# Layer 3's attention of a four-layer transformer stack: two units to a round instead of one

## The reference

```
xn = layer_norm(context) ; ln = layer_norm(latents)          # latents: the normalized x
q  = ln @ Wq                  (8 heads of 64)
k_x, v_x = xn @ Wkv           # k_x is turned by the rotary tables (cos, sin)
k_l, v_l = ln @ Wkv
k, v = concat(k_x, k_l), concat(v_x, v_l)                     # 512 keys
attn = softmax(q k^T / 8)
out  = (attn v) @ Wo
x = x + tanh(g) * out
```

## Time and profile before

| | |
|---|---|
| median of 3 runs | 1868.87 us (1865.15 to 1870.61) |
| the profiled execution's own time | 1862.23 us |
| its span | 1860.5 us |
| TensorE busy | 1693.1 us, 91% of the span |
| VectorE busy | 1091.3 us, 59% |
| ScalarE busy | 681.6 us, 37% |
| mean granted TensorE clock | 0.975 |

### The profile page before, as it was taken

One profiled execution on the slowest core, in us unless ns is written; L12 is line 12 of the kernel. 1 busy time (PEld: TensorE's weight loads), 2 busy tenths in 40 slices (PEclk: granted clock), 3 DMA queues, 4 the chain that ended last, 5 costly groups with the idle time before them and its releaser, 6 DMA issues. The chain is left out here.

```text
span 1860.5 us, 28250 instructions
## 1 busy us (share of the span) xinstructions
PE 1693.1 (91%) x9431; PEld 1236.4 (66%) x9431; DVE 1091.3 (59%) x3250; ACT 681.6 (37%) x1747; POOL 258.4 (14%) x277
## 2 busy tenths in 40 slices
PE   6889778799998999999887799999889999999799
PEld 4667546567766568888676578887656665656575
DVE  5988866568787532232368571002356777676666
ACT  5877842454454211111133222221133443344331
POOL 2100131211022100000232120000120001010115
PEclk9999989999999999999899899999989999999999
DMA  8854042211012325454353875335221111011363
GB/s 250 254 184 134 7 128 68 80 37 36 28 58 81 110 90 170 153 165 169 102 170 117 292 285 176 114 124 176 57 86 43 43 44 50 26 35 29 103 190 113
DMA packets 170926, 212.91 MB, mean 114 GB/s; under 512 B 17081, under 2 KB 137506, under 8 KB 170658
## 3 DMA queue, kind: packets, MB, share of 16 engines
q1 hardware_dynamic: 159730, 183.57, 30.7%
q0 software_dynamic: 10496, 27.28, 4.6%
q10 hardware_dynamic: 560, 0.27, 0.1%
HBM read 148.95 MB, written 57.92 MB: 111 GB/s over the span
## 5 line engine op out<-in xcount | busy, mean ns | idle before, releaser
L788 POOL DMA_INDIRECT slots_in<-f_xn,f_slot x88 | 85.0, 966 | 465.1 <-DVE f_slot L562 441.3
L3506 PE MATMUL r_bank<-r_w,r_hT 128*128 x624 | 139.3, 379 | 1.0 <-DVE r_hT L3650 1.0
L3506 PEld LDWEIGHTS r_bank<-r_w,r_hT 128*128 128x128 f32 x624 | 118.4, 190 | 22.8 <-issue 7.5
L1498 ACT ACTIVATE a_probs<-a_s,a_negmax 128x512 f32<-128x512 f32 x128 | 86.9, 684 | 103.7 <-DVE a_negmax L1746 103.7
L1347 PEld LDWEIGHTS a_t<-kept_ident,a_probs 128*128 128x128 f32 x768 | 83.1, 142 | 61.8 <-issue 38.8
L1331 PE MATMUL a_s<-a_kT,a_qT 64*128 64x256 f32 (+1 forms) x512 | 109.1, 524 | 14.2 <-ACT a_probs L1504 7.6
L3591 DVE TENSOR_TENSOR r_y<-r_bank,r_b_row 128x256 f32<-128x256 f32 (+1 forms) x27 | 14.7, 543 | 177.5 <-PE r_bank L3506 177.2
L3121 PE MATMUL r_bank<-r_xgT,r_firsts 128*128 128x256 f32 x512 | 113.2, 379 | 0.0
L2283 DVE CUSTOM_DVE_ANT_0 a_s<-a_s,a_mask_bias 128x256 f32<-128x256 f32 x256 | 100.5, 454 | 20.3 <-PE a_s L2110 20.1
L1746 DVE TENSOR_REDUCE a_negmax<-a_s 128x1 f32<-128x512 f32 x128 | 82.2, 683 | 49.7 <-PE a_s L1331 49.1
L1347 PE MATMUL a_t<-kept_ident,a_probs 128*128 128x128 f32 x768 | 106.4, 281 | 2.0 <-DVE a_probsT L1764 1.6
(11 more groups left out here) (424 smaller groups left out, 3408.3 us busy)
## 6 DMA issues: line engine op xcount, KB each, us to landing
r_firsts<-in_f_w SPq DMA_DIRECT2D x27, 1024.0 KB, 5.1
r_firsts<-in_f_w SPq DMA_DIRECT2D x46, 512.0 KB, 4.3
slots_in<-a_zeros SPq DMA_DIRECT2D x8, 2048.0 KB, 12.6
half_in<-a_zeros SPq DMA_DIRECT2D x8, 1024.0 KB, 9.7
r_w<-in_f_w SPq DMA_DIRECT2D x8, 1024.0 KB, 7.0
a_share_of<-shares_out SPq DMA_DIRECT2D x28, 256.0 KB, 3.9
r_xg<-slots_in SPq DMA_DIRECT2D x28, 256.0 KB, 2.9
slots_out<-r_y SPq DMA_DIRECT2D x28, 256.0 KB, 2.1
```

Source lines behind the costliest of these rows:

```text
L788: pool.indirect_dma_start(self.slots_in[:, :], bass.IndirectOffsetOnAxis(ap=self.slot[:, c, tile:tile + 1], axis=0), src, None).then_inc(s ...
L1498: last = nc.scalar.activation(probs[:, g % PROBS, i, :], bank[:, :], ACT.Exp, bias=negmax[:, g % 4, i, 0:1], accum_out=sum_of(e, h, t_only))
L3506: last = nc.tensor.matmul(d_bank[:, t * D:(t + 1) * D], hT[:, j % 2, m, t * P:(t + 1) * P], slots.second[:, bass.ds(e, 1), m, :], start=(m ...
```

## The change

In layer 3 two steps make a round. In a round TensorE issues the score products of both units (four in a row), then the turns of both units (s - 2 and s - 1), then the preparations, finishing parts and extras of the first step and of the second, then the value product. VectorE keeps maxima and copies unit by unit (maxima of s, copies of s - 2, maxima of s + 1, copies of s - 1) and does the other jobs of both steps after them. ScalarE does the exponentials of both units first. It gets one wait more: the second unit's exponentials wait for the turn of the unit that used the buffer of probabilities. Bank numbers follow the new order. The table of preparations changes: `rope` from position 1 to 2, `x` from 3 to 2, `v` 0 from 2 to 4 and `v` 1 from 3 to 4, `q` from 4 to 5, `kl` from 5 to 6, `v` 2 from 6 to 7. `x_ask` then lands at position 0 and `norm_x` at 1; the routing's `f_ask` at 0, `f_normed` at 1, `f_turn` at 2. The unit whose copies ScalarE takes over in each batch is unit 1 instead of unit 0. `rotate` moves from position 4 to 6. Choice, gates and count come later by 1, 1 and 2 steps; for the last routed group by 3, 3 and 4, with its tables at steps 64 to 67 instead of 61 to 64. Layer 1 has STRIDE 1 and keeps its order.

```
+    STRIDE = 2 if WIDE else 1
+    SOON_LAG, LOGITS_LAG, EXP_LAG, COUNT_LAG = (2, 4, 6, 3) if WIDE else (1, 3, 4, 2)
-    TURN_AT = U_OF["rope"] + 3 if cfg.rope else None
+    TURN_AT = U_OF["rope"] + 4 if cfg.rope else None
...
-        s = out_step(b) + (ASK_LAG if b < ASKED_SOON else 1)
+        s = out_step(b) + (ASK_LAG if b < ASKED_SOON else SOON_LAG)
...
-        extra[s + 3].append(("f_logits", b, 0))
+        extra[s + LOGITS_LAG].append(("f_logits", b, 0))
...
-        s = out_step(b1 - 1) + (1 if soon else ASK_LAG) + 4
+        s = out_step(b1 - 1) + (SOON_LAG if soon else ASK_LAG) + EXP_LAG
...
+    ROUNDS = [range(s, min(s + STRIDE, STEPS)) for s in range(0, STEPS, STRIDE)]
...
 # TensorE
+            for together in ROUNDS:
+                for s in together:
+                    if s < BATCH * NU:
+                        scores(*divmod(s, NU))
+                for s in together:
+                    if 0 <= s - LAG_T < BATCH * NU:
+                        turn_probs(*divmod(s - LAG_T, NU))
+                for s in together:
+                    b, u = divmod(s, NU)
+                    for kind, e, n in prep_jobs(b, u):
+                        prepare(kind, e, n)
...
+                for s in together:
+                    if 0 <= s - LAG_PV < BATCH * NU:
+                        weigh(*divmod(s - LAG_PV, NU), s)
...
 # ScalarE
+                    if s < BATCH * NU:
+                        if s != together[0] and s >= PROBS:
+                            act.wait_ge(t_full, t_at["pT", (s - PROBS) // NU, ((s - PROBS) % NU, 1)] + 1)
+                        exponent(*divmod(s, NU))
...
 # preparations of layer 3
-             {0: [("c", 0)], 1: [("rope", 0), ("rope", 1)], 2: [("v", 0)], 3: [("x", 0), ("v", 1)],
-              4: [("q", 0), ("q", 1)], 5: [("kl", 0), ("kl", 1)], 6: [("v", 2)], 7: [("v", 3)]},
+             {0: [("c", 0)], 2: [("x", 0), ("rope", 0), ("rope", 1)], 4: [("v", 0), ("v", 1)],
+              5: [("q", 0), ("q", 1)], 6: [("kl", 0), ("kl", 1)], 7: [("v", 2), ("v", 3)]},
```

More of the change, by code:

```diff
@@ L924, in tiled_attention @@
             extra[(e - 2) * NU + 3].append(("x_scale", e, 0))
-    COUNT_LAG = 2
     ON_ACT = {e * NU + U_OF["rope"] + 1 - LAG_T for e in range(1, BATCH)} if cfg.rope else set()
-    TURN_AT = U_OF["rope"] + 3 if cfg.rope else None
+    TURN_AT = U_OF["rope"] + 4 if cfg.rope else None
     ASK_LAG = (X_AT - 2 - LATEST) % NU if head is not None else 1
+    STRIDE = 2 if WIDE else 1
+    SOON_LAG, LOGITS_LAG, EXP_LAG, COUNT_LAG = (2, 4, 6, 3) if WIDE else (1, 3, 4, 2)
     ASKED_SOON = route.cfg.sparse - 1 if route.cfg.sparse < BATCH else route.cfg.last - 1
     for b in range(route.cfg.last):
-        s = out_step(b) + (ASK_LAG if b < ASKED_SOON else 1)
+        s = out_step(b) + (ASK_LAG if b < ASKED_SOON else SOON_LAG)
         extra[s].append(("f_ask", b, 0))
@@ L962, in tiled_attention @@
         number(kind, e, n)
[L963 to L977, removed]
+    for together in ROUNDS:
+        for s in together:
+            b, u = divmod(s, NU)
+            if b < BATCH:
+                s_at["qk", b, (u, 0)] = len(s_at)
+                s_at["qk", b, (u, 1)] = len(s_at)
+            if 0 <= s - LAG_T < BATCH * NU:
+                bb, uu = divmod(s - LAG_T, NU)
+                t_at["pT", bb, (uu, 0)] = len(t_at)
+                t_at["pT", bb, (uu, 1)] = len(t_at)
+        for s in together:
+            b, u = divmod(s, NU)
+            for kind, e, n in prep_jobs(b, u) + finish_jobs(b, u):
+                if kind not in ("share", "inverse"):
+                    number(kind, e, n)
+            for kind, e, n in extra[s]:
+                if kind in ("f_turn", "f_logits", "f_count"):
+                    number(kind, e, n)
     moved_at = {}
@@ L1412, in _ @@
                 pe.wait_ge(v_cleared, 1)
[L1413 to L1441, removed]
@@ new lines, in _ @@
+            for together in ROUNDS:
+                for s in together:
+                    if s < BATCH * NU:
+                        scores(*divmod(s, NU))
+                for s in together:
+                    if 0 <= s - LAG_T < BATCH * NU:
+                        turn_probs(*divmod(s - LAG_T, NU))
+                for s in together:
+                    b, u = divmod(s, NU)
+                    for kind, e, n in prep_jobs(b, u):
+                        prepare(kind, e, n)
+                    for kind, e, t in finish_jobs(b, u):
+                        if kind == "oback":
+                            turn_back(e, t)
+                        elif kind == "sums":
+                            turn_sums(e)
+                        elif kind == "spread":
+                            spread_inverse(e, t)
+                        elif kind == "y":
+                            project_out(e, t)
+                    for kind, e, n in extra[s]:
+                        if kind == "f_turn":
+                            route.tensor_turn(pe, s_turn(s_at[kind, e, n]), e).then_inc(s_full, 1)
+                        elif kind == "f_logits":
+                            if e == 0:
+                                pe.wait_ge(route.consts_in, 16 * len(route.consts))
+                            pe.wait_ge(s_free, s_at["f_turn", e, 0] + 1)
+                            route.tensor_logits(t_turn(t_at[kind, e, n]), e).then_inc(t_full, 1)
+                        elif kind == "f_count":
+                            route.tensor_count(pe, t_turn(t_at[kind, e, n]), n).then_inc(t_full, 1)
+                for s in together:
+                    if 0 <= s - LAG_PV < BATCH * NU:
+                        weigh(*divmod(s - LAG_PV, NU), s)
@@ L1521, in move_turned @@
                     nc.scalar.copy(turned(e, u, i), t_bank(n)[:, :].rearrange("p (k n) -> p k n", k=KT)).then_inc(t_moved, 1)
[L1523 to L1550, removed]
@@ new lines, in _ @@
+            for together in ROUNDS:
+                for s in together:
+                    if s - LAG_T in ON_ACT:
+                        move_turned(*divmod(s - LAG_T, NU))
+                    if s < BATCH * NU:
+                        if s != together[0] and s >= PROBS:
+                            act.wait_ge(t_full, t_at["pT", (s - PROBS) // NU, ((s - PROBS) % NU, 1)] + 1)
+                        exponent(*divmod(s, NU))
+                for s in together:
+                    b, u = divmod(s, NU)
+                    for kind, e, n in prep_jobs(b, u):
+                        if kind in S_KINDS:
+                            move(kind, e, n)
+                    for kind, e, n in extra[s]:
+                        if kind == "x_ask":
+                            norm.take(act, e, e + 1)
+                        elif kind == "x_stats":
+                            norm.take(act, e, e + 2)
+                        elif kind == "f_ask":
+                            route.norm.take(act, e, e + 1)
+                        elif kind == "f_turn":
+                            act.wait_ge(s_full, s_at[kind, e, n] + 1)
+                            route.scalar_turned(s_bank(s_at[kind, e, n]), e).then_inc(s_free, 1)
+                        elif kind == "f_exp":
+                            route.scalar_exp(act, n)
+                        elif kind == "f_count" and route.relu2:
+                            route.scalar_scaled(act, n)
+                for s in together:
+                    done = block_done(s)
+                    if done is not None:
+                        e, blk = divmod(done, BLOCKS)
+                        act.wait_ge(o_full, done + 1)
+                        nc.scalar.copy(o_raw[:, e % 2, blk, :], o_bank[:, 0:SEQ]).then_inc(o_free, 1)
@@ L1737, in _ @@
                     norm_c(e)
[L1738 to L1788, removed]
-                    elif kind == "newest_x":
-                        head.vector_combine(dve, step, e)
-                    elif kind == "x_ask":
-                        norm.ask(step, e, e + 1)
-                    elif kind == "x_stats":
-                        new_stats(e)
-                        new_stats(e + 1)
-                        norm.ask(step, e, e + 2)
-                    elif kind == "x_scale":
-                        norm.scale(dve, step, e, e + 2)
-                    elif kind != "f_turn":
-                        route_job(kind, e, n)
-                for kind, e, t in finish_jobs(b, u):
-                    if kind == "share":
-                        share(e)
-                    elif kind == "spread":
-                        share_spread(e, t)
```

71 lines of the change are left out of this document (added).

## The result

The changed kernel takes 1896.85 us (median of 5, 1894.77 to 1897.77) against 1868.86 (median of 5): ratio 1.0155, 95% interval 1.0143 to 1.0167. It is slower by 28 us; 21 were forecast, as 1890 in a range of 1866 to 1903.

The account below looks back on a forecast made before the run. TensorE was taken to bound the stage (47.4 of 49.1 us per batch). VectorE's queue stalling it (+11.5, seam savings included) and the slow clock (+10.2) gave +21.7 on 1868.9: 1890.6, rounded to 1890, range 1866 to 1903.

Parts of the forecast that it names:

- VectorE's queue in A blocks the fourth turned piece: VectorE's jobs from the batch's first round delay a bank's copy, so round B's last turned piece starts at 14.75 us.
- A: First round of a batch, units 0 and 1; TensorE's work there was to end at 6.4 us.
- stall of 5.2: TensorE's idle time in round B, in two pieces (9.3 to 10.4 and 10.9 to 14.75 us).
- round D: Fourth round of a batch, units 6 and 7; forecast to take 12.6 us, with rotate hidden.
- The slow clock: After round B's stall a lower granted clock slows x and ropes: 1.7 us per batch, 10.2 in batches 1 to 6.
- Seams: Grouping score products and dropping one full-array seam saves TensorE 0.3 us (0.2 to 0.4) per round.
- The turns: Both units' turns in a row on TensorE were to take 1.86 us, no more than 1.9.
- B: Second round of a batch, units 2 and 3, holding four turned pieces, x and ropes; to end at 21.9 us.
- C: Third round of a batch, units 4 and 5; forecast 17.0 us, with VectorE's ropes and share done before it.
- Batches: Batch 1 was to lose 1.5 us and batches 2 to 6 10.0, before the clock's 1.7 for each.
- sign: Period of batches 2, 3 and 5 at 51.5 to 53.5 us in the changed trace would show the forecast right.
- Opening and tail: Batch 0, and last batch to SyncE's last issue: 0 each, bounds -3 to +4 and -5 to +6 us.

Follow-up runs that it names:

- e2: The changed kernel with unit 0's turned copies on ScalarE in each batch instead of unit 1's; 1889.8 us.
- e4: The changed kernel with only the routing's ask, norm and turn moved to positions 5, 6, 7, and choice, gates, count three steps earlier; 1871.1 us.
- e6: The changed kernel with rounds of one step (STRIDE = 1), keeping the new table of preparations and the later routing steps; 1885.7 us.
- e1: The changed kernel with turned pieces repeated into the same bank to keep TensorE busy in its two idle places of round B; 1884.6 us.
- e8: e3 with logits moved to round B and the first two groups' gates to round D; 1856.1 us, ratio 0.9935 against the kernel before.
- e9: e8 without rounds: single steps, old table of preparations, old lags of the last routed group; 1876.0 us, ratio 1.0046 against the kernel before.
- e7: The kernel before, with only newest_x, x_ask and norm_x of batches from 2 on four steps earlier; 1859.3 us, ratio 0.9945.
- e3: e4 with newest_x, x_ask and norm_x of batches from 2 on also four steps earlier, in round C of the batch before; 1877.4 us.

## Why the prediction was right

- *VectorE's queue in A blocks the fourth turned piece.* Right, at 15.07 for 14.75 forecast, with the waits named (3.67 for 3.85 on the copy, 1.33 for 1.1 on the sums). e2 and e4 show that it is the queue. e6 shows that the table alone makes 2.2 us of it per plain batch; with rounds the waits join and cost the clock as well. The prediction's stall of 5.2 is 4.95 by its own two pieces (1.1 and 3.85), and round D adds up to 12.7, not 12.6; neither changes the account.
- *The slow clock.* Right and priced on its own by e1: 12.7 in batches 1 to 6, for 10.2. The term was the smaller of two sightings, 1.7 per batch; the batches lost 1.4 to 2.8, 2.1 on average. That is 2.5 of the 6.6 by which the stage was missed (28.3 for 21.7).
- *Seams.* Score products in a row took 1.92, as in the opening. The turns were mis-sized: x16 takes 2.00 to the next piece (1.86 forecast, 1.9 my upper bound), 0.14 per round. In A and B this adds nothing of its own, since VectorE's queue sets the fourth piece. By the plain batches of e8 and e9 rounds save 0.8 per batch, of which 0.44 is the wait for the bank of the sums (e9 at 1473.52); about 0.1 per round is left of the 0.3 taken.
- *Missed in C.* VectorE's share waits 1.44 for ScalarE's copy of the last outputs, which follows B's value product, and it starts the maxima of C 0.5 late. I had it done before.
- *Batches.* Batch 1 +3.7 for 3.2; batches 2 to 6 +25.1 (276.6 against 251.5) for 10.0 + 8.5. Of the 6.6 between, the clock is 2.6 (11.1 for 8.5). The other 4.0 is there at full clock too: in e1 these batches take 265.5 for 261.5, 0.6 to 1.0 each. It stands in C and D: in batch 2 of the changed kernel C took 17.65 for 17.0 and D 12.77 for 12.6, by the longer turns, a wait of 0.24 in C and v at 3.59 for 3.45, while A and B of e1 took 21.8 for 21.9. So the periods, 54.0 to 57.2, lie outside the 51.5 to 53.5 that were named as a sign; that sign had left the clock out, and with 1.7 for it they were to be 53.2 to 55.2.
- *Opening and tail.* -1.5 and +1.0, for 0 and 0: two errors that nearly cancel. From unit 0 of batch 7 (1742.47) SyncE's last issue ended at 57.7 (1795.19 + 5.02), for 57.0 forecast.

## What to carry to other kernels

When work is regrouped on the engine that is full, lay out the queue of the engine that frees its buffers: sums over a period (35 of 49 us here) hide that its start may hold a long row of jobs without a pause, here 12.9 us (1468.44 to 1481.34 in the changed kernel). A stall of a few us on TensorE can cost a second time by the clock, here 2.6 on top of 5 in batch 2. A bank wait that goes away by giving a copy to another engine can come back at the next ring, as in e2, when the queue behind both is the same. And a gain is to be compared with the best version without the change: e7 has most of e8's.

## What the runs showed of the hardware

Turned pieces of two units in a row take longer than each for itself: 16 transposes 2.00 us from start to the next piece, 8 of them 0.93. Nothing here shows why. An idle time of only 1.22 us was followed by a granted clock of 0.61 in the next 4 us (e3, batch 2), while the same 1.22 in e3's batch 3 and in e4, 1.34 in e4 and three waits of 1.52, 1.33 and 0.73 in e6 were followed by 1.00. What decides between them stays open here. Repeating a transpose into the same bank while waiting kept the clock at 1.00 through a wait of 4 us, in all of batches 1 to 6 (e1). And the same kernel, with the same order of instructions, gained 0.65% on two chips and 0.12%, within its interval of nothing, on a third.
